# Count matrices of a graph kernel turned by transposing DMAs instead of TensorE transposes

## What is computed

```python
h1 = h @ Wn + bn
neigh = segment_sum(h1[src], dst)                 # layer 0, all edges
w = einsum('rb,bio->rio', att, basis)             # layer 1: 2 relations out of 30 bases of 512 x 512
msg = where(edge_type == 0, msgs[0], msgs[1])
agg = segment_sum(msg, row)                       # layer 1 twice, one matrix for each edge type
z = (1 + e) * h + segment_sum(h[src], dst)        # layer 2, five times
out = log_softmax(A @ (x @ weight) + bias)        # layer 3, A holds the edge weights
```

## Time and profile before

| | before |
|---|---|
| median of 3 runs | 2070.17 us (2068.27 to 2072.72) |
| the profiled execution, its own time | 2070.58 us |
| its span, first to last instruction | 2068.6 us |
| TensorE matmul, busy | 1900.6 us, 92% of the span |
| VectorE, busy | 799.5 us, 39% |
| ScalarE, busy | 626.5 us, 30% |
| mean granted TensorE clock | 0.969 of full speed |
| data moved by DMA | 157.54 MB in 47379 packets |

### The profile page before, as it was taken

How to read it: one execution, slowest core, us unless ns; L and a number is a source line. 1 busy time by engine, 2 the same in 40 slices (tenths; PEclk the granted TensorE clock), 3 DMA queues, 4 the chain that set the end, 5 groups by cost and what they waited for, 6 DMA issues and landing times.

```text
span 2068.6 us, 23800 instructions
## 1 busy us (share of the span) xinstructions
PE 1900.6 (92%) x7966; PEld 907.6 (44%) x7978; DVE 799.5 (39%) x1978; ACT 626.5 (30%) x1200; POOL 7.8 (0%) x27
## 2 busy tenths in 40 slices
PE   4878888589999989999999999999999999987998
PEld 2545554353333434444444444444444445433443
DVE  5666677424111162110111223354444544384122
ACT  1544544414666042111211000132232323275100
POOL 1000000000000000000000000000000000000000
PEclk9999999879999969999999999999999999998999
DMA  5889889670100052100000010700000000021011
GB/s 119 219 204 228 218 202 224 180 274 0 36 1 1 0 173 102 41 0 1 1 21 31 31 41 31 307 29 5 21 6 21 6 21 1 16 66 56 21 51 41
DMA packets 47379, 157.54 MB, mean 76 GB/s; under 512 B 9316, under 2 KB 11260, under 8 KB 38816
## 3 DMA queue, kind: packets, MB, share of 16 engines
q1 hardware_dynamic: 42880, 142.28, 23.9%
q10 hardware_dynamic: 4384, 13.78, 1.9%
HBM read 120.38 MB, written 35.65 MB: 75 GB/s over the span
## 4 chain that ended last, share of the span: by engine, by line
PE 78%; DMA 7%; DVE 5%; ACT 4%; issue 2%; DVEq 1%; another core or an unknown queue 1%; SPq 0%; POOL 0%; ACTq 0%; POOLq 0%
PE psum L1195 29%; PE psum L1181 28%; PE psum L1413 6%; DMA hs<-in_L_gnn_basis 6%; PE psum L1264 3%; PE psum L1098 2%; PE psum L1317 2%; PE psum L1364 2%; PE psum L1130 2%; PE psum L1129 1%; ACT adj L878 1%; DMA hs<-in_x 1%; DVE hs L582 1%; DVE hs L584 1%
## 5 line engine op out<-in xcount | busy, mean ns | idle before, releaser
L1195 PE MATMUL psum<-hs,adj 128*128 128x512 f16 x2880 | 643.0, 380 | 0.8 <-DVE hs L689 0.8
L1181 PE MATMUL psum<-wb,xt 128*128 128x512 f32 x1152 | 511.6, 602 | 15.5 <-DVE hs L817 13.4
L1195 PEld LDWEIGHTS psum<-hs,adj 128*128 128x128 f16 x2880 | 280.1, 98 | 354.0 <-issue 37.1
L1181 PEld LDWEIGHTS psum<-wb,xt 128*128 128x128 f32 x1152 | 219.2, 193 | 286.0 <-issue 283.9
L970 ACT ACTIVATE adj<-hs,pbias 128x512 f32<-128x512 f32 x216 | 134.5, 708 | 86.1 <-PE psum L1264 86.1
L1130 PE MATMUL psum<-hs 128*128 128x192 f32 x636 | 159.2, 333 | 0.0
L1003 ACT ACTIVATE ua<-ua 128x512 f32<-128x512 f32 x60 | 37.9, 631 | 335.3 <-DVE ua L831 187.6
L582 DVE TENSOR_SCALAR hs<-hs 128x128 f32<-128x128 f16 x318 | 89.8, 282 | 105.7 <-PE psum L1130 63.1
L1413 PE MATMUL psum<-hs,adj 128*128 128x512 f32 x288 | 123.8, 592 | 0.0
L768 DVE TENSOR_TENSOR vt<-psum,adj 128x512 f32<-128x512 f32 x24 | 16.6, 692 | 271.9 <-PE psum L1181 271.9
L1130 PEld LDWEIGHTS psum<-hs 128*128 128x128 f32 x636 | 117.0, 197 | 7.2 <-issue 1.2
(11 more groups left out here) (213 smaller groups left out, 1478.8 us busy)
## 6 DMA issues: line engine op xcount, KB each, us to landing
hs<-in_L_gnn_basis SPq DMA_DIRECT2D x64, 960.0 KB, 8.2
aw_scratch<-xt ACTq DMA_DIRECT2D x12, 768.0 KB, 5.5
adj<-aw_scratch SPq DMA_DIRECT2D x1, 9216.0 KB, 38.1
x_scratch<-adj SPq DMA_DIRECT2D x24, 256.0 KB, 2.2
hs<-x_scratch SPq DMA_DIRECT2D x24, 256.0 KB, 2.6
ts_scratch<-adj SPq DMA_DIRECT2D x1, 4608.0 KB, 17.9
as_scratch<-adj SPq DMA_DIRECT2D x1, 4608.0 KB, 30.1
adj<-ts_scratch SPq DMA_DIRECT2D x1, 4608.0 KB, 14.5
```

The lines of the kernel that those rows point to most:

```text
L1181: x = pe.matmul(psum[:, bank, :], xt[:, i, k, :], w[:, k, :], start=first and k == 0, stop=last and k == 3)
L1195: x = pe.matmul(psum[:, i % 2 + (4 * half if own else 0), :], adj[:, m, j, P * i:P * i + P], hs[:, t, half, j, :], start=n == 1 or (own an ...
```

## The change

The 24 float16 eviction instructions of shape 128 x 1024, the 24 of shape 128 x 512 and the 288 float16 transposes go. In their place ScalarE issues two transposing DMAs for each block, one for each edge type, of 128 x 1536 float16 elements, from the slot of `typed` straight into `adj`. It does so right after it has evicted the last window of the block, and ahead of that window's side lots; before, the turning began two windows later. It first waits for the end of its own eviction. The turn lots shrink from six to three for a block, one after each of windows 1, 2 and 3, all of them of the weights; the last block has three after the last window. Before it overwrites a slot of `typed`, ScalarE now also waits until that slot's two transposing DMAs have landed, and it waits for all of them before it counts in `built`. The number of bytes computed is the same.

```diff
-                here += [("turn", s, 2 * (q - 1)), ("turn", s, 2 * (q - 1) + 1)]
+                here += [("turn", s, q - 1)]
             if u == NW - 1:
-                here += [("turn", BLOCKS - 1, n) for n in range(6)]
+                here += [("turn", BLOCKS - 1, n) for n in range(3)]
...
-            return lot_of[("turn", s - 2, 5)] + 1
+            return lot_of[("turn", s - 2, 2)] + 1
...
-                elif q == 1:
-
-                    for t in range(2):
-                        x = act.activation(adj[:, 1 + t, a, (1 - t) * 1024:(1 - t) * 1024 + 512],
-                                           bank.bitcast(F16)[:, t * 512:t * 512 + 512], ACT.Copy)
-                    x.then_inc(side_out, 1)
-                elif q < 3:
-                    act.activation(adj[:, 1 + q // 2, a, q // 2 * 512:q // 2 * 512 + 1024],
-                                   bank.bitcast(F16), ACT.Copy).then_inc(side_out, 1)
...
+            def turn_types(s):
+
+                act.wait_ge(*evicted(PER * s + PER - 1))
+                for t in range(2):
+                    act.dma_start_transpose(adj[:, 1 + t, s, :].rearrange("p (j n) -> p j n", j=NT),
+                                            typed[:, s % 2, t, :, :].rearrange("p j n -> p (j n)")).then_inc(typed_turned[s % 2], 16)
...
                 if u == 0 and s >= 2:
                     act.wait_ge(side_ps, staged_again(s))
+                    act.wait_ge(typed_turned[s % 2], 32 * (s // 2))
                     act.wait_ge(typed_summed, s - 1)
...
+                if u == PER - 1:
+                    turn_types(s)
                 for lot in by_window[w]:
                     side_lot(*lot)
 
+            for k in range(2):
+                act.wait_ge(typed_turned[k], 16 * BLOCKS)
             act.drain().then_inc(built, 1)
...
-                    if q < 3:
-                        for m in range(8):
-                            t, j = divmod(8 * q + m, NT)
-                            x = pe.transpose(bank.bitcast(F16)[:, P * m:P * m + P], typed[:, a % 2, t, j, :], ident16[:])
-                    else:
-                        for m in range(4):
-                            x = pe.transpose(bank[:, P * m:P * m + P], aw_stage[:, a % 2, 4 * (q - 3) + m, :], ident[:])
+                    for m in range(4):
+                        x = pe.transpose(bank[:, P * m:P * m + P], aw_stage[:, a % 2, 4 * q + m, :], ident[:])
```

More of the change, by code:

```diff
@@ L185, in program @@
         win_free = [sem(f"win_free{b}") for b in range(RING)]
-        typed_summed = sem("typed_summed")
+        typed_summed, typed_turned = sem("typed_summed"), [sem(f"typed_turned{k}") for k in range(2)]
         row_out = sem("row_out")
@@ L870, in side_lot @@
                     act.activation(ua[:, c % 2, :], bank, ACT.Copy).then_inc(side_out, 1)
-                elif q == 1:
-                    for t in range(2):
-                        x = act.activation(adj[:, 1 + t, a, (1 - t) * 1024:(1 - t) * 1024 + 512],
-                                           bank.bitcast(F16)[:, t * 512:t * 512 + 512], ACT.Copy)
-                    x.then_inc(side_out, 1)
-                elif q < 3:
-                    act.activation(adj[:, 1 + q // 2, a, q // 2 * 512:q // 2 * 512 + 1024],
-                                   bank.bitcast(F16), ACT.Copy).then_inc(side_out, 1)
                 else:
-                    if q == 3:
+                    if q == 0:
                         act.wait_ge(row_out, 16 * (a + 1))
-                    act.activation(aw_row[:, 512 * (q - 3):512 * (q - 2)], bank, ACT.Copy).then_inc(side_out, 1)
-                    if q == 5:
+                    act.activation(aw_row[:, 512 * q:512 * (q + 1)], bank, ACT.Copy).then_inc(side_out, 1)
+                    if q == 2:
                         act.wait_ge(side_out, side_copied(n))
                         act.dma_start(aw_dram[:, a, :], aw_row).then_inc(row_out, 16)
+            def turn_types(s):
[3 more added lines that the diff above has]
+                                            typed[:, s % 2, t, :, :].rearrange("p j n -> p (j n)")).then_inc(typed_turned[s % 2], 16)
             def move_keys(n):
```

## The result

The changed kernel takes 2173.03 us (median of four runs, 2141.65 to 2178.46), against 2071.44 us before in the same comparison: ratio 1.0411, 95% interval 1.0288 to 1.0534. The ratio leaves out two of the four runs, 2175.12 and 2178.46 us, which count as disturbed, so it rests on 2141.65 and 2170.94 us, its interval is wide, and it gives a smaller loss, 85 us (60 to 111), than the difference of the medians, 101.6 us. The profile is of the run of 2178.46 us, with a span of 2176.6. The direction forecast is right; the time is near the upper end of the range, 90 us from the forecast 2083, and outside the range of the forecast's own case, 2070 to 2110.

What follows compares the result with a forecast made beforehand. The prediction took DMA transfers and in-order engines to bound the build phase almost equally. Transfers +10, ScalarE's queue +4 and the phase's end -2 gave +12 us on 2070.58: 2083 us, range 2052 to 2180.

Steps and rivals of the forecast that it cites:

- the forecast's own case: Build phase: each transposing transfer takes 1.3 to 3 us of engine time, total 2070 to 2110 us; chance 0.44.
- What bounds the phase: Build phase: DMA transfers and in-order engines limit it nearly equally, each leaving room of 32 us from 347 to 315 us.
- Engine time of a transposing DMA: Build phase, 24 added DMAs: 1.0 to 5.7 us each, taken as 1.66 us, 40 us together.
- The sum: Whole kernel: +10 us for transfers, +4 for ScalarE's queue, -2 at the phase's end, +12 us on 2070.58.
- The middle row: Build phase: each transposing DMA runs at the rate of q1, mostly basis loads, 0.237 MB in a us: 1.66 us.
- The second rival: Build phase: turning cuts transfers into 256-byte packets, 59 ns each, 5.7 us a transfer, total 2190 us; chance 0.20.
- rivals 2 and 3: Build phase: small packets, 2190 us, chance 0.20; turning one 128 x 128 tile at a time, 2223 us, chance 0.09.
- ScalarE's queue: Build phase: two issues a block at 0.33 us delay the basis eviction and next load; 8 us, half counted, +4 us.
- Tile after tile: Build phase: turning passes one unit, a 128 x 128 tile at a time, 1.6 us each, total 2223 us; chance 0.09.
- The first rival: Build phase: the transfers fit into holes of the DMA stream, so faster, 2061 down to 2036 us, taken 2056; chance 0.27.
- The phase's end: Last weight row before SyncE's release: ready some 3 us sooner but behind two transposing DMAs; -2 us, range -3 to +4.
- The clock: Build phase, TensorE: clock at 0.99, none to be won; more waiting for loads could lose some.

Runs made afterwards that it cites:

- e1: Changed kernel with the two transposing DMAs of a block as plain copies of the same bytes, nothing turned: 2077.5 us, ratio 1.0027 to before.
- e6: Kernel before with basis loads cut to 64 of 2048 elements a row from the third chunk on, bases wrong: 2042.0 us, against 2074.2 before.
- e2: Changed kernel with plain copies cut into 256-byte runs, 1536 packets a matrix, instead of transposing DMAs: 2093.8 us, ratio 1.0103 to before.
- e7: Changed kernel with basis loads cut to 64 of 2048 elements a row from the third chunk on, bases wrong: 2024.6 us.
- e11: Changed kernel with transposing DMAs and basis loads kept apart in time by waits on ScalarE and SyncE: 2126.1 us, ratio 1.0272 to before.
- e4: e1 plus six dummy ScalarE instructions, some 7 us, behind each block's copies: 2095.6 us, 18 us over e1.
- e13: Changed kernel with each basis load cut into four DMAs of 2 KB a row instead of one of 8 KB: 2074.6 us.
- e8: Kernel before with a block's six turn lots one after each of windows 1 to 6, not two after each of 1 to 3: 2040.9 us.
- e12: Kernel before with each basis load cut into four DMAs of 2 KB a row instead of one of 8 KB: 2050.7 us.

## Why the prediction was right in direction and short in size

- **What bounds the phase: right.** The transfers and the in-order engines are limits of nearly equal height. e1 shows that relief of the engines brings nothing while 31 us of copies are added, e6 that relief of the transfers alone brings 32 us. That the waits for loads would grow, that the DMA engines would be full to the phase's end (0.98), that line 878's waits would go and that the layers wouldn't change, all came so.
- **Engine time of a transposing DMA: the step that failed.** The sum took 1.66 us, between 1.0 and 5.7; the trace after gives 4.9. The middle row was q1's mean rate, bytes over time, and it would have been right for a plain copy, for which e1 measures 1.3 us and 5 us of loss against the +12 of the sum. Of the 3.6 us above that, 1.2 are small packets (e2, 2.5 us), and 2.4 are time in which turned packets stand beside the loads; alone, the same DMA takes 2.1 to 2.3 us (e7, e11). The sum also left the old transfers at their 299 us. The loads' queue took 68.0% of 461 us, 313, instead of 274 for the same bytes: 39 us that had no term.
- **The second rival gave the time, 2190 us from 5.7 us each, for a reason that is only partly right.** The 1536 packets are there, and q10's share from 34 to 495 us, 29.8%, is its "near 30". But at 26 ns a packet they explain 16 of the 95.5 us. Its 59 ns is the mean of 18 packets with 0.01 MB together, from a share with one digit; the usual packet of 256 bytes took 18 ns. That its total comes out near is luck. The measured time lies in the range only because the range reaches past 2110 us for rivals 2 and 3.
- **An assumption that stood in the sum unsaid** was that two queues share the engines in proportion, as the weight row and the loads do. It held for plain transfers and not for these. The prediction's last paragraph names it as what would make it wrong: engines taken out of service beyond the transfer's own bytes.
- **ScalarE's queue: right place, wrong size.** +4 us was counted from 0.33 us an issue; it is 1.3 us at best and 12 at worst, and worth some 20 us by e4. "More if a turned transfer takes longer to describe" was there, without a number.
- **Tile after tile: ruled out.** Twelve tiles land in 4.1 us where no load disturbs them, 0.34 us a tile. The Trainium skill, VectorE: DVE Perf Modes, The three transpose paths, has 1309 ns for one; without loads beside it no run here shows that much, and the measurement decides. Beside the loads a DMA's median landing, 13.7 us, is 1.1 us a tile, for another reason.
- **The first rival, faster, is true where its condition holds**: with no loads beside it the change wins 17.4 us. Its point of decision, 1.3 us of engine time, fits e1, which has 1.3 us and lies within 5 us of before.
- **The phase's end: a small miss.** From ScalarE's eviction of the last window (386.07 us before, 494.79 after) to the loads of `x` it is 9.1 us in both. The -2 us didn't come: the two last issues hold ScalarE for 3.4 us, and the weight lots' evictions wait behind them.
- **The clock** was named as something that could be lost and put at nothing. It fell from 0.99 to 0.85 in the phase; its share of the loss is open.

The Trainium skill says in Advanced Engine Details and Errata, X-Bar Transpose (TRN2), that transposing DMAs are as fast as regular ones. Here a matrix takes 2.1 to 2.3 us of the engines when alone, against 1.3 for a plain copy beside loads or 2.5 for one in the same packets of 256 bytes, and 4.9 beside loads. So the traces agree where packets are equal and nothing stands beside, and not against long packets or beside loads; there the measurement decides. The same section speaks of wavefronts of 16 rows. If all engines must bring a row of such a group together, an engine that is busy with an 8 KB packet holds up the other fifteen, and that would give what e7, e11 and e13 show. This mechanism is argued, not shown; shown is that the loss needs both kinds of traffic at once, that single packets of both then stand for microseconds, and that it shrinks when the loads are cut into shorter pieces.

What stays open: which of the two, the engine's order of queues or the joint arrival, makes the packets wait; whether the second DMA of a pair costs more than the first, and why; whether a load's packets or its length as one DMA count; what the lower clock costs; and how e8's order and e12's cut add up, which wasn't tried.

## What to carry to other kernels

A transfer's price beside another stream isn't its bytes or its packets alone: before turning is moved to DMA, look at whether long transfers from memory run at the same time, for the same instructions saved 17 us without them and cost 85 to 102 us with them. Where turning DMAs must run beside loads, cut the loads into shorter pieces or keep both apart, and don't spread the turning over more of the load stream. And where two limits are of equal height, look first at the order of work that makes holes in both: six lots one by one instead of in pairs brought 1.4%, with no other edit.

## What the runs showed of the hardware that was not expected

- A transposing DMA of 128 x 1536 float16 elements is 1536 packets of 256 bytes and 32 more; its issue holds ScalarE's queue at least 1.3 us, and up to 12.0 us beside the loads. A plain copy in 256-byte runs holds it as well, 0.6 to 5.2 us.
- Alone it lands in 3.8 to 4.3 us; beside loads of 8 KB rows in 5.0 to 28.6 us, and a load beside it in up to 29.8 us instead of 11.2. For 6 us the engines were 0.67 busy at 37 GB/s. Over the whole run one turned packet in twenty took over 200 ns, while the median stayed at 18 ns.
- Loads of the bases as four DMAs of 2 KB rows instead of one of 8 KB rows, the same bytes, make the kernel 0.9% quicker; q1's share falls from 23.9% to 21.7% of the span.
